# Cross-attention with layer norm on one core: a weight load moved ahead of an input, the first query product moved between two folds, and half of the layer norm moved to other engines

## The reference

```python
# B = 8 batches, 256 query rows (width 256), 256 key rows (width 192), H = 8 heads of D = 256
Q = x @ Wq;  K = ctx @ Wk;  V = ctx @ Wv                 # split into heads
score = einsum('bhqd,bhkd->bhqk', Q, K) / sqrt(D)        # masked by atten_mask
attn  = softmax(score)
out   = (attn @ V, heads side by side) @ Wo + x
mu, var = mean(out), var(out)                            # over the last axis
result = (out - mu) * rsqrt(var + 1e-5) * gamma + beta
```

## Time and profile before

| | |
|---|---|
| median of 3 runs | 315.33 us (315.28 to 315.57) |
| the profiled execution | 315.15 us, its span 313.3 us |
| PE busy | 306.4 us, 98% of the span |
| VectorE (DVE) busy | 253.2 us, 81% |
| ScalarE (ACT) busy | 221.7 us, 71% |
| GpSimd (POOL) busy | 181.5 us, 58% |
| mean granted TensorE clock | 0.995 of full |
| memory read, written | 32.24 MB, 17.83 MB |
| the chain that ended last | PE 95%, DMA 2%, DVE 1%, SP's queue 1% |

### The profile page before, as it was taken

The page is one execution under the profiler, slowest core; times in us unless marked ns, Lnnn a source line. Parts: engine busy times, 40 slices in busy tenths (PEclk is TensorE's granted clock), DMA queues, the critical chain, the costliest instruction groups (busy, mean ns, idle before and its releaser), DMA issues.

```text
span 313.3 us, 8037 instructions
## 1 busy us (share of the span) xinstructions
PE 306.4 (98%) x2574; PEld 299.9 (96%) x2574; DVE 253.2 (81%) x721; ACT 221.7 (71%) x601; POOL 181.5 (58%) x183
## 2 busy tenths in 40 slices
PE   8999999999999999999999999999999999999993
PEld 7998888999999999999999999999999999999992
DVE  0467778778999879988998889988998899985786
ACT  2446677778877887678777797678767887777640
POOL 1123476556864587558864586458755686458212
PEclk9999999999999999999999999999999999999998
DMA  7996444463353653574445555364455446440101
GB/s 256 363 406 240 138 134 152 143 218 122 87 178 124 212 166 118 175 238 147 134 126 184 162 165 154 141 224 134 135 189 160 148 154 184 139 156 9 36 0 67
DMA packets 46911, 50.27 MB, mean 160 GB/s; under 512 B 3504, under 2 KB 37040, under 8 KB 46896
## 3 DMA queue, kind: packets, MB, share of 16 engines
q1 hardware_dynamic: 46608, 49.56, 47.9%
q10 hardware_dynamic: 288, 0.52, 0.7%
HBM read 32.24 MB, written 17.83 MB: 160 GB/s over the span
## 4 chain that ended last, share of the span: by engine, by line
PE 95%; DMA 2%; DVE 1%; SPq 1%; issue 0%; POOLq 0%; POOL 0%
PE score_bank L328 24%; PE out_bank L328 19%; PE gL_bank L328 14%; PE tL_bank L328 14%; PE tU_bank L328 9%; PE gU_bank L328 7%; DMA wq_raw<-in_wqT 2%; PE spare_bank L328 1%; PE spare_bank L362 1%; PE tL_bank L362 1%; PE tL_bank L344 1%; PE tU_bank L344 1%; PE out_bank L368 1%; PE tU_bank L368 1%; PE out_bank L344 0%; PE spare_bank L344 0%
## 5 line engine op out<-in xcount | busy, mean ns | idle before, releaser
L1038 POOL TENSOR_TENSOR probs<-probs,inv_sum 128x512 f32<-128x512 f32 x64 | 66.7, 1043 | 82.2 <-DVE inv_sum L824 81.9
L633 ACT ACTIVATE probs<-neg_scores,neg_max 128x256 f32<-128x256 f32 x128 | 64.1, 502 | 36.9 <-DVE neg_max L813 36.9
L1061 POOL TENSOR_TENSOR pT_lo<-pT_raw,pT_hi 128x512 fp32r<-128x512 f32 x60 | 76.8, 1303 | 8.6 <-ACT pT_hi L589 8.6
L813 DVE CUSTOM_DVE_ANT_0 neg_scores<-score_bank,mask_bias 128x256 f32<-128x256 f32 x128 | 49.1, 420 | 5.5 <-PE score_bank L328 3.0
L834 DVE STREAM_TRANSPOSE squares<-probs 128x512 f32<-128x512 f32 x60 | 42.4, 706 | 2.9 <-DMA scratch<-squares 2.6
L589 ACT ACTIVATE tL_hi<-tL_bank 128x512 fp32r<-128x512 f32 x31 | 18.6, 599 | 26.5 <-PE tL_bank L328 26.4
L328 PE MATMUL gL_bank<-xT_hi,A_hi 128*128 128x256 f32 x128 | 35.3, 276 | 0.0
L328 PE MATMUL gL_bank<-xT_lo,A_hi 128*128 128x256 f32 x128 | 35.3, 276 | 0.0
L328 PE MATMUL gL_bank<-xT_hi,A_lo 128*128 128x256 f32 x128 | 35.3, 276 | 0.0
L589 ACT ACTIVATE pT_hi<-pT_raw 128x512 fp32r<-128x512 f32 x60 | 34.3, 622 | 0.0
L328 PE MATMUL out_bank<-CL_lo,tL_hi 128*128 128x256 f32 x118 | 32.6, 276 | 0.0
(11 more groups left out here) (176 smaller groups left out, 997.7 us busy)
## 6 DMA issues: line engine op xcount, KB each, us to landing
scratch<-squares SPq DMA_DIRECT2D x30, 512.0 KB, 3.2
pT_raw<-scratch SPq DMA_DIRECT2D x120, 128.0 KB, 3.1
xT_raw<-in_xT SPq DMA_DIRECT2D x8, 256.0 KB, 4.6
ctxT_raw<-in_ctxT SPq DMA_DIRECT2D x8, 256.0 KB, 4.8
wo_raw<-in_wo SPq DMA_DIRECT2D x4, 512.0 KB, 13.6
x_res<-in_x SPq DMA_DIRECT2D x8, 256.0 KB, 3.2
out<-y SPq DMA_DIRECT2D x7, 256.0 KB, 2.7
wq_raw<-in_wqT SPq DMA_DIRECT2D x3, 512.0 KB, 7.5
```

Of the source, the lines that this page charges most:

```text
L633: nc.scalar.activation(probs[j % 2][:, n, :], neg_scores[:, n, :], ACT.Exp, bias=neg_max[:, n:n + 1], scale=-1.0, accum_out=row_sum[:, n:n ...
L813: nc.vector.tensor_tensor_reduce(out=neg_scores[:, n, :], in0=score_bank[hh][:, q, :], in1=mask_bias[:], scale=-SCALE, scalar=3.0e38, op0= ...
L1038: nc.gpsimd.tensor_tensor(probs[j % 2][:, rows, :], probs[j % 2][:, rows, :], inv, ALU.mult) \
L1061: nc.gpsimd.tensor_tensor(pT_lo[j % 2][:, k].rearrange("p hh (q i r) -> p (hh q) i r", q=QT, i=ROWS), pT_raw[j % 2][:, k].rearrange("p i n ...
```

## The change

Four edits:

- SyncE loads xT of batch 0 behind the weights of pair 1 instead of ahead of them.
- TensorE makes query 0 between folds 3 and 4 instead of between folds 5 and 6; ScalarE and VectorE follow that order (ScalarE: query 0's g behind head 3, the copies of heads 4 and 5 behind it, then ctxT, heads 6 and 7).
- In the loop the second half of the layer norm is computed as ((y * rstd - mean * rstd) * gamma) + beta. GpSimd makes mean * rstd and its negative (`shift_by_mean`: two operations of two columns) behind `deviation`; ScalarE makes y * rstd + shift, one operation for each tile (`standardise`), at the end of its step j = 0; GpSimd multiplies by gamma and adds beta (`affine`: two operations on 128 x 512) at the end of its step j = 0. VectorE's `centre` and `normalise` leave the loop.
- The last two batches keep VectorE's way, with counters of their own (`y_tail_scaled`, `y_tail_done`).

```diff
@@ SyncE
             def store_out(b):
-                sp.wait_ge(y_out_done, QT * b + QT)
+                if isinstance(b, int) and b == B - 2:
+                    sp.wait_ge(y_tail_done, QT)
+                else:
+                    sp.wait_ge(y_out_done, b + 1)
                 sp.dma_start(batch_of(out, b), y[:]).then_inc(out_stored, 16)
@@ the loads: the end of the passes over pairs
+                if j == 1:
                     load_xT(0)
@@ TensorE
-            for h in range(H - 2):
+            for h in range(H // 2):
                 fold_A(h)
             pe.wait_ge(A_split, 4)
             query_products(0, 0, 0)
-            for h in range(H - 2, H):
+            for h in range(H // 2, H):
                 fold_A(h)
@@ ScalarE
+            def standardise(b):
+                act.wait_ge(shift_done, b + 1)
+                for q in range(QT):
+                    nc.scalar.activation(y[:, q, :], y[:, q, :], ACT.Identity, bias=shift[:, q:q + 1],
+                                         scale=rstd[:, q:q + 1]).then_inc(y_scaled_done, 1)
...
                 if not (isinstance(t, int) and t < LAG - 1):
                     pT_hi_part(t - LAG + 1, (j - LAG + 1) % PAIRS)
+                if ends is not None:
+                    standardise(ends)
...
             xT_hi_part(0)
-            for h in range(2, H - 2):
+            for h in range(2, H // 2):
                 A_hi_part(h)
             gU_hi_part(0)
             gL_hi_part(0)
+            for h in range(H // 2, H - 2):
+                A_hi_part(h)
             ctxT_hi_part(0)
@@ VectorE, in a step
-                if ends is not None and j == 0:
-                    centre(ends)
                 gU_lo_part(t + 1, 0)
                 gU_lo_part(t + 1, 1)
                 gL_lo_part(t + 1)
                 if by_squares:
                     transpose_squares(t, j, 1)
-                if ends is not None and j == 0:
-                    normalise(ends)
@@ GpSimd
+            def shift_by_mean(b):
+                pool.wait_ge(rstd_done, b + 1)
+                nc.gpsimd.tensor_tensor(scaled_mean[:], mean_var[:, :, 0], rstd[:], ALU.mult) \
+                    .then_inc(scaled_mean_done, 1)
+                pool.wait_ge(scaled_mean_done, b + 1)
+                nc.gpsimd.tensor_tensor(shift[:], zeros[:, 0:QT], scaled_mean[:], ALU.subtract).then_inc(shift_done, 1)
+            def over_rows(row):
+                return row[:].rearrange("p (o d) -> p o d", o=1).broadcast_to((P, QT, DI))
+            def affine(b):
+                pool.wait_ge(y_scaled_done, QT * b + QT)
+                nc.gpsimd.tensor_tensor(y[:], y[:], over_rows(gamma_sb), ALU.mult).then_inc(y_gained, 1)
+                pool.wait_ge(y_gained, b + 1)
+                nc.gpsimd.tensor_tensor(y[:], y[:], over_rows(beta_sb), ALU.add).then_inc(y_out_done, 1)
@@ GpSimd, in a step
                 if ends is not None:
                     deviation(ends)
+                    shift_by_mean(ends)
...
                     pT_lo_part(t - LAG + 1, (j - LAG + 1) % PAIRS)
+                if ends is not None:
+                    affine(ends)
@@ GpSimd, ahead of the loop
+            pool.wait_ge(affine_in, 32)
```

More of the change, by code:

```diff
@@ L114, in attention_kernel @@
         rstd = sb("rstd", [P, QT])
+        scaled_mean = sb("scaled_mean", [P, QT])
+        shift = sb("shift", [P, QT])
         y_last = probs[0][:, 0:QT, :]
@@ L204, in attention_kernel @@
         var_eps_done = sem("var_eps_done")
+        scaled_mean_done = sem("scaled_mean_done")
+        shift_done = sem("shift_done")
         rstd_done = sem("rstd_done")
         y_scaled_done = sem("y_scaled_done")
+        y_gained = sem("y_gained")
         y_out_done = sem("y_out_done")
+        y_tail_scaled = sem("y_tail_scaled")
+        y_tail_done = sem("y_tail_done")
         waits_passed = sem("waits_passed")
@@ L316, in _ @@
             for q in range(QT):
-                sp.wait_ge(y_out_done, QT * (B - 1) + 1 + q)
+                sp.wait_ge(y_tail_done, QT + 1 + q)
                 sp.dma_start(out[B - 1][:, q, :], y_last[:, q, :]).then_inc(out_stored, 16)
@@ L686, in tU_hi_part, with step @@
                 hi_part(places("tU", t)[1], tU[:]).then_inc(t_hi_done, 1)
-            def step(t, j, b, folds=()):
+            def standardise(b):
[3 more added lines that the diff above has]
+                                         scale=rstd[:, q:q + 1]).then_inc(y_scaled_done, 1)
+            def step(t, j, b, ends=None, folds=()):
                 before = not (isinstance(t, int) and t < OUT_LAG)
@@ L730, in _ @@
                 step(PAIRS * b + 3, 3, b)
-                step(PAIRS * b + 4, 0, b + 1)
+                step(PAIRS * b + 4, 0, b + 1, ends=b - 1)
                 step(PAIRS * b + 5, 1, b + 1)
@@ L891, in centre_tile @@
                     rows[:, q, :], rows[:, q, :], mean_var[:, q, 0:1], gamma_sb[:],
-                    ALU.subtract, ALU.mult).then_inc(y_scaled_done, 1)
+                    ALU.subtract, ALU.mult).then_inc(y_tail_scaled, 1)
             def normalise_tile(b, q, rows):
-                dve.wait_ge(y_scaled_done, QT * b + q + 1)
+                dve.wait_ge(y_tail_scaled, QT * (b - B + 2) + q + 1)
                 nc.vector.scalar_tensor_tensor(
                     rows[:, q, :], rows[:, q, :], rstd[:, q:q + 1], beta_sb[:],
[L899 to L912, removed]
+                    ALU.mult, ALU.add).then_inc(y_tail_done, 1)
             def step(t, j, b, ends=None, folds=()):
@@ L967, in _ @@
                 step(PAIRS * b + 3, 3, b, ends=b - 1)
-                step(PAIRS * b + 4, 0, b + 1, ends=b - 1)
+                step(PAIRS * b + 4, 0, b + 1)
                 step(PAIRS * b + 5, 1, b + 1)
@@ L988, in _ @@
             pT_lo_part(STEPS - 1)
-            centre(B - 2)
+            dve.wait_ge(mean_done, QT * (B - 1))
+            for q in range(QT):
+                centre_tile(y, q)
             t_lo_part_lower(STEPS - 2)
@@ L995, in _ @@
             t_lo_part_upper(STEPS - 1)
-            normalise(B - 2)
+            dve.wait_ge(rstd_done, B - 1)
+            for q in range(QT):
+                normalise_tile(B - 2, q, y)
             for q in range(QT):
```

## The result

The changed kernel takes 314.82 us (median of 20 runs), the one before 315.42 in the same comparison: ratio 0.998, 95% interval 0.9974 to 0.9986. That is 0.60 us less, against 0.57 forecast (314.76). The sign and the size came out; several steps behind them did not, as the trace shows.

The account below looks back on a forecast made before the run. TensorE was taken to bound nearly everything, with only pair 1's weight arrival winnable: 0.73 us won, part lost at query 0, leaving 0.57; loop and tail 0. Profiled 315.15 became 314.58, plus 0.18 for the median: 314.76, range 314.35 to 315.4.

Parts of the forecast that it names:

- six sevenths: Share of the kernel, 52 to 285 us, in which only TensorE's own work was said to take time.
- The term of 0.66 us for 256 KB: Head loads: moving xT's 256 KB behind pair 1, at 390 KB per us, brings pair 1 0.66 us sooner.
- 8.26: Head: forecast landing time in us of pair 1's weights, 8.92 less 0.66.
- The new wait at query 0: Head, TensorE: query 0 waits some 0.23 us for the xT split, taking back part of a 0.73 us gain.
- the four times of the head: Forecast signs: fold 2 at 8.3 to 8.4, xT's copy at 9.0, query 0 at 11.0, step 0's scores at 18.5.
- the missing wait for wq_raw: Head, forecast sign: fold 2 starts at 8.3 to 8.4 us without waiting for pair 1's wq_raw.
- The 0.02 that turned 0.55 into 0.57: Head, TensorE: allowance for a slightly quicker restart after a wait, raising the forecast gain from 0.55 to 0.57 us.
- Rival 4: Loop or early steps give the gain back, by stalls of some 0.1 us or a load-bound step: 315.3 us; chance 0.06.
- The forecast of 0: Loop: moving the layer norm's second half off VectorE gains 0, bounds -0.1 and +0.3 us per iteration.
- the bound by the port rule: Loop: VectorE's upper split, held for a whole 1.04 us GpSimd operation, ends at 134.1, before TensorE's use at 134.38.
- The limit of "over 4 us" for the pair: Loop: GpSimd's two new 128x512 operations delay VectorE's transposes and then TensorE only if together over 4 us.
- rival 3: Loop: ScalarE's new function reloads its table, 1.28 us each, two per iteration, 4.8 us in all, 319.6 us; chance 0.03.

Follow-up runs that it names:

- e1: Only the two head edits (xT behind pair 1, query 0 earlier) on the kernel before, layer norm left on VectorE: 314.87 us, ratio 0.998.
- e2: Only the layer norm edit on the kernel before, head unchanged: 315.19 us, ratio 0.9996.
- e6: Changed kernel plus one more unread 128x512 gamma product on GpSimd per iteration, between the new pair: 314.86 us, ratio 0.9988.
- e7: Changed kernel plus two more unread 128x512 gamma products on GpSimd per iteration, between the new pair: 323.01 us, ratio 1.0239.
- e8: Changed kernel unaltered, run once more for a second profile of its start: 315.13 us.
- e10: Changed kernel with VectorE's low parts of g ahead of both transposes in steps 0 to 3: 314.80 us, ratio 0.9978.
- e9: Kernel before with VectorE's low parts of g ahead of both transposes in steps 0 to 3: 315.47 us, ratio 0.9996.
- e3: Only xT loaded behind pair 1 on the kernel before, query 0 still between folds 5 and 6: 315.13 us, ratio 0.9988.
- e4: Only query 0 moved between folds 3 and 4 on the kernel before, xT still ahead of pair 1: 315.38 us, ratio 0.9995.
- e12: Changed kernel with pair 1 loaded by heads, VectorE's low parts ahead of transposes, layer norm back on VectorE: 314.49 us, ratio 0.9967.
- e5: Changed kernel with pair 1's weights loaded by heads (head 2, xT, head 3): 314.55 us, ratio 0.9974.

## Why the prediction was right

**The bound.** Right: pair 1's weights are what ends last at the start, TensorE what fills the rest, and the head alone carries the gain (e1, e2). But the stretch of the earlier trace rows is 233 of 313.3 us, three quarters of the span and not six sevenths; the second bound, at 41 us, lies in the part that it leaves out.

**The arrival.** The term of 0.66 us for 256 KB was right: 0.62 over ten profiles, 0.66 over eleven. Its place was wrong: 8.26 was counted from the 8.92 of the earlier trace rows, which was an early arrival (fold 2 started at 9.04 to 9.56 in the other three profiles with xT ahead). Fold 2 started at 8.65 behind a wait of 0.63 us, where I had it at 8.34 without one.

**The fold before it.** I took fold 1's start at 7.04 as fixed. It is 6.13 to 7.04 in the profiles, the kernel before being the latest. So the forecast was limited by TensorE on one side (0.62 to fold 2) and by the late query on the other, while in most profiles TensorE is through with fold 1 at 7.4 to 8.3 and waits for pair 1 with xT on either side of it.

**The new wait at query 0.** Right in kind and size: TensorE was ready at 10.06 + 1.16 = 11.22 and started at 11.43, 0.21 against 0.23. The times are 0.4 later than forecast (11.43 for 11.03, 18.89 for 18.48), as xT landed with the rest: its copy started at 9.31, not 9.0. Of the signs named beforehand, the four times of the head thus all came 0.3 to 0.4 late, and the missing wait for wq_raw was there. The 0.02 that turned 0.55 into 0.57 has a row of its size: query 0's second matmul follows its first by 0.20 us behind the wait (11.43 to 11.63), by 0.25 without one (14.13 to 14.38 before).

**Why the sum held all the same.** In the two profiles step 0's scores are only 0.14 us apart, and the ends 0.25. Measured over runs it is 0.60, since the profile before was faster than its median by 0.27 (315.15 to 315.42), the one after slower by 0.08 (314.90 to 314.82). The forecast of 0.57 was made of a right transfer time and two starts that were both untypical, with errors that cancel. That is luck in the parts; what carried it is the transfer time, since all behind the arrival shifts with it: over the profiles step 0's scores start at 19.29 in the mean with xT ahead (four) and at 18.77 with both edits of the head (after, e1, e6, e7, e8, e10), 0.52 sooner.

**What I missed.** The pause of 0.10 us at 41.22 in the chain before. Rival 4 ("a step that was bound by a load") names the kind; it is a store, and it took back 0.46 us in the second profiled execution of the changed kernel (292.04 less 291.58).

**The loop.** The forecast of 0 stands: from step 0's scores to the last operation it is 291.57 and 291.58 us with the layer norm moved (e2, after), 291.55 to 291.57 with it on VectorE (e9, e1, e3, e4, e12). The prices were less good. The pair on GpSimd took 2.59 us, at the upper bound and not at 1.04 each; ScalarE's two operations 1.08 instead of 0.85, more than the 1.0 named as their most and than the 1.02 idle, but the copy behind them starts at 128.44, 0.24 sooner than before like TensorE's own work. The margin at tU's split grew from 0.25 to 0.72 us, by less than the 0.9 by which VectorE was to be sooner: the split starts 1.01 sooner, but beside GpSimd's normalisation it takes 0.91 us instead of 0.62, and TensorE itself is 0.25 sooner. It ended at 133.41, where the bound by the port rule was 134.1. The store of y was issued at 133.64 and not held up. The limit of "over 4 us" for the pair is bracketed: 3.9 us are free (e6), with 5.2 TensorE waits (e7).

**The port rule.** The Trainium skill (SBUF — State Buffer, Who interferes with whom) has a VectorE operation with two SBUF inputs and a GpSimd operation that reads SBUF take turns. In e7 the split of 98.89 ends at 100.29, 0.28 behind the GpSimd operation that ends at 100.01 (97.33 + 2.68), after 1.40 us instead of 0.43: the trace agrees. So do the splits beside the normalisation, which end 0.28 behind it in the kernel before (134.13, 133.85) and 0.27 behind it in the changed one (133.41, 133.14). They don't show turns of whole operations: a split held to the end of the other and then run whole would end 0.43 behind it. It is one more way in which work moved to GpSimd comes back to VectorE: the operations that left it had 12.7 us in the stretch from 52 to 285 us, but its busy time fell by 9.2 only, and the upper splits of t went from 630 to 702 ns in the mean, 2.0 us in all.

**The function table.** The changed kernel's trace has one load of it, at 1.66 us, and none in the loop: rival 3 didn't happen. ScalarE: Activation LUTs of the Trainium skill (Table sets: the hidden batching unit) has identity in every set, and the trace agrees.

## What to carry to other kernels

When a kernel is bound by one engine nearly everywhere, look for the arrival that it waits for first, then at once for the next one behind it, down to pauses of 0.1 us in the chain: a gain ends there. Don't build absolute times on one profiled start: here the first loads' arrival varied by 0.6 us and the first fold by 0.9, as much as the effect; differences (bytes by rate) held. Compare the spacing of the bounding engine's steps too, and not only its waits: in e7 a wait of 0.6 us stands at the head of slower steps that cost 7 us without a further wait, whether it brought them on or not.

## What the runs showed of the hardware

- One wait of 0.6 us of TensorE at 104 us in e7 was followed by steps of 8.95 us instead of 8.61 (matmuls of 256 columns every 0.118 us instead of 0.113) for the rest of the loop. The granted clock was shown as 1.00 (2.4 GHz) in 52 to 285 us, as in the other runs. The slower spacing isn't e7's own: the changed kernel has 0.118 in query 0 (11.63 to 13.51 us) and in the first 3 us of step 0, and 0.113 in the 3 us behind. New in e7 is that it lasts. Waits at step 3, before the loop, weren't followed by lasting slower steps (e5, e8, and e7 itself, with 8.61 us a step until the wait at 104). The cause stays open; no run here tells it apart.
- A GpSimd product of 128x512 with a broadcast operand took 1.04 us where one value serves a whole row of 256 (probs by inv_sum) and 1.29 where a row of 256 values is read for each tile (y by gamma), as long as with three full operands (1.27 to 1.30).
- A store of 512 KB took 3.4 to 5.8 us in step 1 (3.4 in e9, 5.8 in e7), while transposed probs were being loaded, and 2.6 in the median of the changed kernel.
